# Output projection as seven Strassen block products, with x reloaded for the residual and streamed in pieces

## The reference, cut to what matters

```python
q = einsum('bchw,dc->bdhw', x, theta_w) + theta_b          # d = 256
xpool = maxpool2(x)                                        # 16 x 16 pixels
k = einsum('bchw,dc->bdhw', xpool, phi_w) + phi_b
v = einsum('bchw,dc->bdhw', xpool, g_w) + g_b
p = softmax(einsum('bdn,bdm->bnm', q, k) * 256 ** -0.5)
vp = einsum('bdm,bnm->bdn', v, p)
return einsum('bdhw,cd->bchw', vp, z_w) + z_b + x
```

## Time and profile before

| | us |
|---|---|
| median of three runs | 2207.38 |
| the profiled execution's own time | 2208.27 |
| its span in the trace | 2206.5 |
| PE busy | 2171.7 |
| DVE busy | 1466.0 |
| POOL busy | 918.0 |
| ACT busy | 852.1 |
| HBM traffic | 138.42 MB read, 134.22 MB written |

### The profile page before, as it was taken

The page is one execution under the profiler, slowest core; times in us unless marked ns, Lnnn a source line. Parts: engine busy times, 40 slices in busy tenths (PEclk is TensorE's granted clock), DMA queues, the critical chain, the costliest instruction groups (busy, mean ns, idle before and its releaser), DMA issues.

```text
span 2206.5 us, 32144 instructions
## 1 busy us (share of the span) xinstructions
PE 2171.7 (98%) x11520; PEld 1855.6 (84%) x11520; DVE 1466.0 (66%) x2355; ACT 852.1 (39%) x1521; POOL 918.0 (42%) x386
## 2 busy tenths in 40 slices
PE   6999999999999999999999999999999999999997
PEld 5788888888888888888888888888888888888885
DVE  7676666776666766667766667666677666676655
ACT  5344333344333443433433334434334333344331
POOL 4453343543434533435434345334354343443420
PEclk9999999999999999999999999999999999999999
DMA  6233334323234233343232342333433323423323
GB/s 229 77 113 117 119 113 149 135 104 142 100 128 152 107 121 116 113 152 130 108 143 95 133 152 105 124 114 114 152 125 112 140 98 133 152 105 124 114 77 114
DMA packets 143266, 272.91 MB, mean 124 GB/s; under 512 B 8592, under 2 KB 11664, under 8 KB 143248
## 3 DMA queue, kind: packets, MB, share of 16 engines
q1 hardware_dynamic: 143104, 272.66, 34.1%
q10 hardware_dynamic: 144, 0.01, 0.0%
HBM read 138.42 MB, written 134.22 MB: 124 GB/s over the span
## 4 chain that ended last, share of the span: by engine, by line
PE 96%; issue 1%; DVE 1%; ACT 1%; DMA 0%; POOL 0%; POOLq 0%; SPq 0%; ACTq 0%
PE bank L475 96%; DVE z_lo L356 0%; DVE pooled L365 0%; DMA x<-theta_wt 0%; DVE theta_lo L356 0%; POOL pt_lo L342 0%; ACT x_split_hi L244 0%; ACT q_hi L256 0%; POOLq L70 0%; ACT g_hi L237 0%; ACT pt_hi L315 0%; DVE xp_lo L417 0%; ACT xp_hi L248 0%; DVE att_lo L385 0%; DVE x L402 0%
## 5 line engine op out<-in xcount | busy, mean ns | idle before, releaser
L330 POOL TENSOR_TENSOR x_split_lo<-x,x_split_hi 128x1024 fp32r<-128x1024 f32 x256 | 617.5, 2423 | 872.6 <-ACT x_split_hi L244 869.8
L402 DVE SCALAR_TENSOR_TENSOR x<-bank,bias,x 128x512 f32<-128x512 f32 x512 | 383.2, 749 | 184.3 <-PE bank L475 184.1
L394 DVE STREAM_TRANSPOSE pt_raw<-probs 32x256 f32<-32x256 f32 x1024 | 446.8, 436 | 44.0 <-ACT probs L309 26.9
L475 PE MATMUL bank<-x_split_hi,theta_hi 128*128 128x512 f32 x1024 | 405.3, 396 | 10.3 <-POOL x_split_lo L330 10.3
L475 PE MATMUL bank<-x_split_lo,theta_hi 128*128 128x512 f32 x1024 | 409.9, 400 | 0.0
L475 PE MATMUL bank<-att_hi,z_hi 128*128 128x512 f32 x1024 | 405.4, 396 | 2.6 <-DVE att_lo L385 1.7
L475 PE MATMUL bank<-att_lo,z_hi 128*128 128x512 f32 x1024 | 405.5, 396 | 0.0
L475 PE MATMUL bank<-att_hi,z_lo 128*128 128x512 f32 x1024 | 405.1, 396 | 0.0
L475 PE MATMUL bank<-x_split_hi,theta_lo 128*128 128x512 f32 x1024 | 402.3, 393 | 0.0
L244 ACT ACTIVATE x_split_hi<-x 128x1024 fp32r<-128x1024 f32 x256 | 269.6, 1054 | 171.2 <-PE bank L475 166.7
L365 DVE TENSOR_REDUCE pooled<-x 128x256 f32<-128x1024 f32 x256 | 310.4, 1214 | 16.4 <-DMA x<-x 14.0
(11 more groups left out here) (51 smaller groups left out, 3420.7 us busy)
## 6 DMA issues: line engine op xcount, KB each, us to landing
x<-x SPq DMA_DIRECT2D x256, 512.0 KB, 5.6
out<-x SPq DMA_DIRECT2D x256, 512.0 KB, 2.8
x<-theta_wt SPq DMA_DIRECT2D x4, 256.0 KB, 7.1
x<-phi_wt SPq DMA_DIRECT2D x4, 256.0 KB, 10.1
x<-g_wt SPq DMA_DIRECT2D x4, 256.0 KB, 8.3
x<-z_wt SPq DMA_DIRECT2D x4, 256.0 KB, 7.1
bias<-biases ACTq DMA_DIRECT2D x1, 7.0 KB, 2.3
```

What stands on the lines that cost most here:

```text
L330: nc.gpsimd.tensor_tensor(xs[LO][:, ks, :], xb[s % BUFS][:, ks, :], raw(xs[HI][:, ks, :]), ALU.subtract).then_inc(x_ready, 1)
L394: last = nc.vector.transpose(dst, src)
L402: nc.vector.scalar_tensor_tensor(out=tile, in0=o_bank[i % 4][:, :], scalar=bias[:, Z_B + i:Z_B + i + 1], in1=tile, op0=ALU.add, op1=ALU.ad ...
L475: last = nc.tensor.matmul(dst, stationary(a), moving(b), start=start and n == 0, stop=stop and n == len(PRODUCTS) - 1)
```

## The change

1. The output projection, z (1024 x 256) by att (256 x 512), is cut into 2 x 2 blocks: z into four of 512 x 128, att into four of 128 x 256. It is computed as seven block products in the Winograd form of Strassen's scheme (P1 to P7). A block product is four tiles of 128 channels by three matmuls of 256 columns.
2. The sums of z blocks (S1 to S4, and the negated A22) are made once, in step 0. The sums of att blocks (T1 to T4) are made for each half by POOL (`difference`); ACT writes att to `att_f` (`copy_att`), then splits seven blocks in three groups (`hi_att`), and POOL makes all their remainders (`lo_att`).
3. The block sums of the result are made partly in PSUM (a later product accumulates on an earlier one) and partly by DVE: seven adds of two instructions each (`add`, line 615, 14 a half) onto an x that is loaded a second time, to `x_top` (two buffers) and `x_bot` (one buffer). ACT adds z_b to these tiles, eight instructions a half (`bias_top`, `bias_bot`).
4. x for the projections comes in quarter halves through a ring of six buffers (`xb`), and its splits through a ring of three (`xs`).
5. On PE the four q pieces stand between the products, K is computed at the end of an odd step ahead of the attention product, V behind the scores of the next, even step. K goes to bank 2, V to bank 6.
6. The loop body has six steps in place of four; two steps stand ahead of the loop, eight behind it. z weights are no longer awaited ahead of step 0 but in step 1.

```diff
+SPLITS = ((B11, T3), (T1, T4 + 1), (T3, T1))
+P1, P2, P6, P5, P7, P3, P4 = range(7)
+A_TOP, U_TOP, C11, V_BOT, C22, C12, C21 = range(7)
...
-        xb = [sb(f"x{i}", [P, KT, H], f32) for i in range(BUFS)]
-        xs = [sb(f"x_split_{s}", [P, KT, H], f32r) for s in ("hi", "lo")]
+        xb = [sb(f"x{i}", [P, KC, H], f32) for i in range(XB)]
+        xs = [[sb(f"x_split_{s}{i}", [P, KC, H], f32r) for s in ("hi", "lo")] for i in range(XS)]
+        x_top = [sb(f"x_top{i}", [P, TB, H], f32) for i in range(2)]
+        x_bot = sb("x_bot", [P, TB, H], f32)
...
-        o_bank = [bank[6], bank[7], bank[2], bank[3]]
-        k_bank, v_bank = bank[6], bank[7]
+        k_bank, v_bank = bank[2], bank[6]
+        o_y, o_v, o_x = bank[2:4], bank[4:6], bank[6:8]
...
+            def load_bot(turn, s):                                  # SP
+                for j in range(2):
+                    if begun(turn, s, 1):
+                        sp.wait_ge(bot_stored[j], upto(turn, s, 16, 0))
+                    else:
+                        sp.wait_ge(z_ready, 7)
+                    sp.dma_start(x_bot[:, 2 * j:2 * j + 2, :], ...).then_inc(bot_loaded[j], 16)
...
             def step(turn, s):                                      # SP
+                load_top(turn, s)
+                if begun(turn, s, 1):
+                    load_bot(turn, s - 1)
+                if exists(turn, s, 3):
+                    for c in range(CH):
+                        load_x(turn, s + 3, c)
+                if begun(turn, s, 1):
                     store(turn, s - 1)
...
+            def blocks(turn, s):                                    # POOL
+                pool.wait_ge(att_copied, upto(turn, s, DT, DT))
+                difference(T1, B12, B11)
+                pool.wait_ge(t_done, upto(turn, s, 4, 1))
+                difference(T2, B22, T1)
+                lo_att(turn, s, 0)
+                pool.wait_ge(t_done, upto(turn, s, 4, 2))
+                difference(T4, T2, B21)
+                difference(T3, B22, B12)
...
-                    nc.vector.scalar_tensor_tensor(out=tile, in0=o_bank[i % 4][:, :], scalar=bias[:, Z_B + i:Z_B + i + 1],
-                                                   in1=tile, op0=ALU.add, op1=ALU.add).then_inc(o_ready, 1)
+            def add(turn, s, which):                                # DVE
+                group, source, rows, cols = ((P1, o_x, 0, 0), (P6, o_x, 0, 1), (P2, o_y, 0, 0), (P5, o_v, 1, 1),
+                                             (P7, o_x, 1, 1), (P3, o_v, 0, 1), (P4, o_x, 1, 0))[which]
+                for j in range(2):
+                    dve.wait_ge(o_done, upto(turn, s, SUMS, 2 * group + j + 1))
...
+                    nc.vector.tensor_tensor(tiles, source[j][:, :].rearrange("p (i n) -> p i n", n=HB), tiles,
+                                            ALU.add).then_inc(o_added, 1)
...
+            def step_first(turn, s):                                # DVE, step 0
...
+                for b in range(P // Q):
+                    transpose_probs(turn, s, b)
+                sum_z()
+                pool_ahead(turn, s, 2)
+                pool_ahead(turn, s, 3)
+                lo_z()
+                lo_q(turn, s + 1)
...
+            def project_out(turn, s, group):                        # PE
...
+                for j in range(2):
+                    if reads is not None:
+                        pe.wait_ge(o_added, upto(turn, s, SUMS, 2 * reads + j + 1))
+                    for i in (2 * j, 2 * j + 1):
+                        last = product(banks[j][:, (i % 2) * HB:(i % 2 + 1) * HB], lambda a: zw[a][:, zi, i * P:(i + 1) * P],
+                                       lambda b: att[b][:, bi, :], opens and i % 2 == 0, True, True)
+                    last.then_inc(o_done, 1)
...
+            def step(turn, s):                                      # PE
+                scores(turn, s)
+                if begun(turn, s, 2):
+                    pe.wait_ge(o_added, upto(turn, s - 1, SUMS, 0))
+                if s % 2 == 0 and begun(turn, s, 1):
+                    project_v()
+                project_q(turn, s + 1, 0)
...
+                project_out(turn, s - 1, P1)
+                project_q(turn, s + 1, 1)
+                pe.wait_ge(exp_done, upto(turn, s, NT, NT))
+                project_out(turn, s - 1, P2)
+                project_out(turn, s - 1, P6)
+                project_q(turn, s + 1, 2)
+                project_out(turn, s - 1, P5)
+                project_out(turn, s - 1, P7)
+                project_q(turn, s + 1, 3)
+                project_out(turn, s - 1, P3)
+                project_out(turn, s - 1, P4)
+                if s % 2 and exists(turn, s, 1):
+                    pe.wait_ge(xp_ready, upto(turn, s, 1, 3))
+                    pe.wait_ge(o_added, upto(turn, s - 1, SUMS, 2 * C11 + 1))
+                    project_k()
+                attend(turn, s)
```

More of the change, by code:

```diff
@@ L231, in _ @@
+            load_bot(TURNS, last)
+            store(TURNS, last)
+            for j in range(2):
+                sp.wait_ge(top_stored[j], IMAGES * 32)
+                sp.wait_ge(bot_stored[j], HALVES * 16)
         @block.scalar
@@ new lines, in step_even @@
+            def step_even(turn, s):
+                max_scores(turn, s)
+                pool_ahead(turn, s, 0)
+                invert(turn, s)
+                pool_ahead(turn, s, 1)
+                lo_v(image_of(turn, s))
+                transpose_probs(turn, s, 0)
+                transpose_probs(turn, s, 1)
+                add(turn, s - 1, A_TOP)
+                transpose_probs(turn, s, 2)
+                transpose_probs(turn, s, 3)
+                add(turn, s - 1, U_TOP)
+                add(turn, s - 1, C11)
+                pool_ahead(turn, s, 2)
+                add(turn, s - 1, V_BOT)
+                add(turn, s - 1, C22)
+                pool_ahead(turn, s, 3)
+                add(turn, s - 1, C12)
+                lo_q(turn, s + 1)
+                add(turn, s - 1, C21)
@@ new lines, in step_odd @@
+            def step_odd(turn, s):
+                max_scores(turn, s)
+                pool_ahead(turn, s, 0)
+                invert(turn, s)
+                pool_ahead(turn, s, 1)
+                add(turn, s - 1, A_TOP)
+                transpose_probs(turn, s, 0)
+                pool_ahead(turn, s, 2)
+                pool_ahead(turn, s, 3)
+                add(turn, s - 1, U_TOP)
+                transpose_probs(turn, s, 1)
+                add(turn, s - 1, C11)
+                add(turn, s - 1, V_BOT)
+                transpose_probs(turn, s, 2)
+                add(turn, s - 1, C22)
+                transpose_probs(turn, s, 3)
+                add(turn, s - 1, C12)
+                if exists(turn, s, 1):
+                    lo_q(turn, s + 1)
+                add(turn, s - 1, C21)
+                if exists(turn, s, 1):
+                    lo_k(image_of(turn, s, 1))
@@ L466, in _, with step, product @@
+            def step(turn, s):
+                if not begun(turn, s, 1):
+                    step_first(turn, s)
+                else:
+                    (step_even, step_odd)[s % 2](turn, s)
             steps(dve, step)
-            lo_att(TURNS, BUFS - 1)
-            finish(TURNS, BUFS - 1, range(KT))
+            last = FIRST + PERIOD + PERIOD // 3 - 1
+            for which in range(7):
+                add(TURNS, last, which)
         @block.tensor
         def _(pe):
-            def product(dst, stationary, moving, start, stop):
+            def product(dst, stationary, moving, start, stop, reopens=False):
@@ new lines, in attend @@
+            def attend(turn, s):
+                pe.wait_ge(v_ready, image_of(turn, s, 1))
+                pe.wait_ge(pt_ready, upto(turn, s, 1, 1))
+                for m in range(DT):
+                    if begun(turn, s, 1):
+                        pe.wait_ge(o_added, upto(turn, s - 1, SUMS, 2 * C12 + m + 1))
+                    for mt in range(MT):
+                        last = product(a_bank[m][:, :], lambda a: vt[a][:, mt, m * P:(m + 1) * P],
+                                       lambda b: pt[b][:, mt, :], mt == 0, mt == MT - 1)
+                    last.then_inc(a_done, 1)
```

538 lines of the change are left out of this document (337 added, 201 removed).

## The result

The changed kernel takes 2168.71 us (median of 4 runs, 2164.45 to 2174.61) against 2207.45 of the kernel before: ratio 0.9827, interval 0.9802 to 0.9853. The forecast was 2150.5 us, its range 2127 to 2188. The profiled execution took 2164.45 us, its span is 2162.6.

The account below looks back on a forecast made before the run. PE, busy 98% of the span, was taken to bound the kernel. Span 2206.5 - 74 (projection) + 13 (start) + 4 (end) = 2149.5 us, giving a forecast time of 2150.5 us, range 2127 to 2188.

Parts of the forecast that it names:

- the fetch rival: Loop's end: longer body doesn't stay, each of 8 jumps waits for a transfer, 18 us in all, 2169 us; chance 0.15.
- The projection: Output projection: 84 matmuls of 256 columns at 119 ns, 10.0 us against 11.19; 74 us less over 62 steps.
- the far bound of the term (-84): Output projection's largest gain over the 62 middle steps: 84 us, if its matmuls take 117 ns.
- Is PE still without a wait?: Middle steps: every cover of PE's stages holds by 0.7 us or more, so waits there were put at zero.
- The tightest cover: K to scores: k needs 2.1 us of splitting behind attention's 2.80 us, so it fits by 0.7 us.
- `x_bot`'s load: Second x load into the single buffer: store 2.8, load 5.6 us, ready about 12 us into the step, due at 17.
- The start: Ahead of half 1's scores: z sums and `z_lo` on DVE hold them up, +13 us (+2 to +22).
- The end: Last step and last half: products wait on ACT and POOL, adds follow; +4 us (0 to +8).
- No hand-over was missed: Rival, between engines: a short cover missed by 0.5 us in each step, 32 us, 2182 us; chance 0.12.
- DVE didn't become the bound: Rival, adds on DVE: beside POOL they take 2.53 us each, DVE needs 42 us a step, 2690 us; chance 0.04.
- The matmuls didn't wait for their own loads: Rival, block products: each matmul waits for its own load, 188 ns, 4.6 us more a step, 2500 us; chance 0.03.
- my straight line between the two figures: Matmul distance by the skill's page: 256 columns cost 0.75 of 512, making products slower than before; within a 0.03 chance.

Follow-up runs that it names:

- straight line: Changed kernel with PE's instructions for all 64 steps written one after the other, no loop on PE: 2124.67 us, ratio 0.963.
- Experiment 8: zq_pe with unused tiles that move other tiles' SBUF addresses, no instruction changed; four variants: 2146.01, 2148.62, 2110.32 and 2108.97 us.
- zq_pe: Changed kernel with PE's stream written out and, in step 0, q's splits ahead of the z splits on ACT and DVE: 2122.19 us, ratio 0.9616.
- Experiments 1 to 4: Changed kernel with PE's or every engine's stream written out (2124.67, 2125.56 us) or 12-step body (2133.24); kernel before with 8-step body (2225.18) or 256-column projection (2226.59).
- experiment 5: Changed kernel, PE's stream written out, with three needless maxima on DVE ahead of `k_lo`: one run of 2182.57 us.
- Experiment 6: The run zq_pe: q's splits ahead of z's in step 0, against the changed kernel with PE's stream written out: 2122.19 us, ratio 0.9616.
- experiment 4: The run o256: kernel before with its output projection in 96 matmuls of 256 columns in place of 48 of 512: 2226.59 us, ratio 1.0099.
- o256: Kernel before with its output projection in 96 matmuls of 256 columns in place of 48 of 512: 2226.59 us, ratio 1.0099.
- b8: Kernel before with 8 steps in the loop body in place of 4: 2225.18 us, ratio 1.0097.
- p12: Changed kernel with 12 steps in the loop body in place of 6, so 3 jumps back in place of 8: 2133.24 us, ratio 0.9662.

## Why the prediction was right, and where it wasn't

The sign, the mechanism of the gain and the range held: the span is 13.1 us above the one forecast (2162.6 against 2149.5). That small miss is luck: it is two larger ones against each other. For the same reason the 2169 us of the fetch rival fits the 2168.71 measured so well: its 18 us were 40.9, and the sum that they were added to was 25 us too long.

- **The projection (-74 us forecast): right in kind, too small.** The step that failed is "I lean to the upper rows and take 119 ns". The block products went at 113.7 ns, outside the 117 to 120 of the rows, so 84 of them take 9.55 us and not 10.0. The middle without jumps is 1992.9 us (straight line), 99.4 less than in the earlier trace rows and 25.4 below the forecast. Even the far bound of the term (-84) was too small a gain, since I took 117 ns, the fastest stage seen, for an end. Experiment 8 shows that the address makes the difference between 113.7 and 118 to 119 ns, so the rows of K, V and scores were no sure neighbours: in the kernel before their operands stand as in zq_pe's column, at 96/0, 0/96 and 96/96, and those of the products at 64/0.
- **The fetch at the loop's end: the rival that I gave 0.15 happened, and at 40.9 us in place of 18.** The trigger was told rightly (about 120 packets forecast, 132 seen). The step that failed is "PE has the attention product's 2.80 us queued ahead of the jump, which covers 2.3". The cover was there and even longer, 3.41 us. But 2.3 us was the time of a small transfer, and PE's branch to a body that isn't held took 4.7 to 6.2 us, so 1.5 to 3.1 us of each stood uncovered. And the sum knew of one wait a jump; the block behind the first isn't there either (gaps of 0.5 to 2.3 us), and six of the eight jumps were followed by 3.4 us at half clock. Experiments 1 to 4 show the cause from both sides: taken out of this kernel, and put into the other in two ways.
- **Is PE still without a wait? Right.** Outside the jumps no stage is longer than its matmuls. The adds took 0.69 us, 0.75 forecast. DVE's busy time a step is 24.5 us (26.0 forecast), ACT's 20.2 (20.4), POOL's 21.5 (21.0). The tightest cover, forecast at 0.7 us, was 0.86 in the trace (`k_lo` ended at 304.23, scores were due at 305.09), and experiment 5 overran it by what was expected. `x_bot`'s load took 7.8 us and not 5.6 at a DMA share of 58%, its store 4.7 and not 2.8; the 5 us of slack held both.
- **The start: +8.7 us, +13 forecast.** Half 1's scores start at 78.33 us. PE waits 12.0 us for `q_lo` as told, and `z_lo` beside POOL cost 2.69 us for three of seven, where the forecast had four. `phi_lo`, which has gone beside POOL's splits, took 2.00 us in place of 0.68. Experiment 6 shows that the order there is worth about 3.6 us, not the 8 by which the wait for `q_lo` shrinks: the rest moves to the first products.
- **The end: +5.8 us, +4 forecast.** It lies inside 0 to +8.
- **The rivals that didn't come.** No hand-over was missed. DVE didn't become the bound: an add from PSUM beside POOL keeps 0.69 us, where two SBUF inputs cost 2.0 to 2.7. The matmuls didn't wait for their own loads: 113.7 ns with loads recorded at 189. Half the columns cost 0.487 in experiment 4, where my straight line between the two figures of the Trainium skill ("TensorE: Matmul & The Clock Gate", Back-to-back issue gap) gave 0.75; this case does not agree with it.
- **Slips in the working.** The add time from which the kernel would be slower than before is about 1.29 us by the prediction's own numbers (57 us over 64 steps of 14 adds, on top of 1.22), not 1.35, and the chances of the cases, with the 0.02 for a larger miss, add up to 1.02. Neither touches the forecast.

## What to carry to other kernels

When a change makes a loop's body longer, count the instructions of the body on each engine before and after, and look at the instruction queue's packets: a body that was held and isn't any more costs at every jump, as the length of the engine's branch shows, and a faster body can lose more than it gains (o256). Then write the stream out or use fewer, longer turns. And where hundreds of short matmuls set the time, try the SBUF addresses of their operands with unused tiles of a few dozen bytes: they add no instruction, and they moved this kernel by 12 to 13 us down or 26 up. An experiment that adds a tile should keep the others where they were.

## What the runs showed of the hardware

- PE bodies of 1500 instructions ran 15 turns with 11 packets, and a branch back took 0.21 to 0.24 us; bodies of 1884, 2724, 2996 and 5445 were fetched anew in each turn, with branches of 3.6 to 6.2 us. A jump back cost 2.2 to 6.0 us of PE time, made of what the branch takes beyond the queued matmuls (1.6 us of them in o256 and b8, 3.4 in the changed kernel) and, in the changed kernel and p12, a second wait 4.6 to 5.9 us later; straight fetching of 1.79 MB showed no wait.
- The granted clock fell to 0.5 for 3.4 us after the first gap of six jumps (2.1 to 2.9 us long), and stayed at full after first gaps of 1.4 and 1.6 us, after second gaps of up to 2.3 us, and after all of p12's (up to 1.5 us). The length of the gap alone does not decide it: in b8 and o256 it fell after five gaps of 1.95 to 2.6 us and stayed at full after others of 1.95 to 2.8.
- The distance of 256-column matmuls was 113.2 to 119.9 ns, and changed by up to 6.6 ns a matmul with the SBUF address of an operand alone; at 512 columns it stayed within 231.6 and 234.2 ns.
